# Two-layer graph network: first row tile normalized alone, first head's W1 as two transfers, edge transposes moved to the front

## What is computed

```python
h = jnp.maximum(_layernorm(x, axis=-1), 0.0)
x = x + _L0_gnn_ref(h, edge_index, L0_gnn_W1, ...)   # 4 heads of 512, attention, W2
h = jnp.maximum(_layernorm(x, axis=-1), 0.0)
x = x + _L1_gnn_ref(h, L1_gnn_W1, ..., edge_index)   # graph convolution
...
def _gat_layer(x, src, dst, W, a_src, a_dst, bias, concat):
    h = (x @ W).reshape(N, H, C)
    ...
```

## Time and profile before

| | |
|---|---|
| time, median of 3 runs | 1191.17 us |
| lowest, highest of the 3 | 1186.42 us, 1191.92 us |
| the profiled execution, its time | 1188.23 us |
| its span, from first to last instruction | 1186.5 us |
| TensorE busy | 1114.7 us, 94% of the span |
| VectorE busy | 836.6 us, 71% |
| ScalarE busy | 513.0 us, 43% |

### The profile page before, as it was taken

How to read it: one execution, slowest core, us unless ns; L and a number is a source line. 1 busy time by engine, 2 the same in 40 slices (tenths; PEclk the granted TensorE clock), 3 DMA queues, 4 the chain that set the end, 5 groups by cost and what they waited for, 6 DMA issues and landing times. The chain is left out here.

```text
span 1186.5 us, 17506 instructions
## 1 busy us (share of the span) xinstructions
PE 1114.7 (94%) x7124; PEld 1045.2 (88%) x7124; DVE 836.6 (71%) x1390; ACT 513.0 (43%) x1052; POOL 30.4 (3%) x40
## 2 busy tenths in 40 slices
PE   5999999999999999999999999739999899999998
PEld 5878886789989998999999999729999899889998
DVE  7998896899768886788768778679856623341263
ACT  4232322375547654556547654155445613431120
POOL 4200001020000000000000000000000000000000
PEclk9999999989999999999999999969999999999999
DMA  6133130021011100201020100013002300000321
GB/s 221 66 113 116 40 122 18 1 63 54 1 51 40 54 1 1 89 16 40 1 69 22 54 1 1 1 56 115 28 27 68 116 1 1 27 14 1 131 75 56
DMA packets 27618, 58.44 MB, mean 49 GB/s; under 512 B 3492, under 2 KB 6152, under 8 KB 27536
## 3 DMA queue, kind: packets, MB, share of 16 engines
q1 hardware_dynamic: 27344, 56.96, 14.5%
q10 hardware_dynamic: 192, 0.32, 0.1%
HBM read 41.73 MB, written 15.54 MB: 48 GB/s over the span
## 5 line engine op out<-in xcount | busy, mean ns | idle before, releaser
L1330 PE MATMUL banks<-hs,ring_hi 128*128 128x258 f32 (+1 forms) x1600 | 299.4, 288 | 2.8 <-DVE z L997 2.8
L1330 PEld LDWEIGHTS banks<-hs,ring_hi 128*128 128x128 f32 (+1 forms) x1600 | 247.9, 188 | 4.2 <-DVE z L997 3.0
L1330 PE MATMUL banks<-hs,ring_lo 128*128 128x258 f32 (+1 forms) x800 | 227.0, 284 | 0.0
L248 ACT ACTIVATE e<-banks,al 128x256 f32<-128x256 f32 (+1 forms) x500 | 193.9, 491 | 22.4 <-PE banks L233 22.4
L1330 PEld LDWEIGHTS banks<-hs,ring_lo 128*128 128x128 f32 (+1 forms) x800 | 150.9, 189 | 0.0
L256 ACT ACTIVATE ring_hi<-pf 128x512 fp32r<-128x512 f32 (+1 forms) x125 | 81.6, 653 | 159.8 <-DVE pf L267 156.6
L1358 PE MATMUL banks<-w_hi,oT_hi 128*128 128x384 f32 (+1 forms) x320 | 109.5, 342 | 12.7 <-DVE rows L1025 6.9
L265 DVE TENSOR_TENSOR e<-e 128x512 f32<-128x512 f32 (+1 forms) x125 | 84.5, 676 | 36.6 <-ACT e L248 36.4
L1358 PE MATMUL banks<-w_lo,oT_hi 128*128 128x384 f32 (+1 forms) x320 | 109.0, 341 | 0.0
L1358 PE MATMUL banks<-w_hi,oT_lo 128*128 128x384 f32 (+1 forms) x320 | 108.9, 340 | 0.0
L1204 PE MATMUL banks<-w_hi,xT_hi 128*128 128x512 f32 x240 | 97.4, 406 | 0.5 <-DVE w_lo L781 0.5
(11 more groups left out here) (262 smaller groups left out, 2109.7 us busy)
## 6 DMA issues: line engine op xcount, KB each, us to landing
h_scratch<-stage SPq DMA_DIRECT2D x30, 256.0 KB, 2.0
hs<-h_scratch SPq DMA_DIRECT2D x30, 256.0 KB, 2.9
w_st<-in_L_gnn_W SPq DMA_DIRECT2D x4, 1536.0 KB, 7.4
w_st<-in_L_gnn_W SPq DMA_DIRECT2D x16, 384.0 KB, 3.5
gw_st<-in_L_gnn_W SPq DMA_DIRECT2D x12, 384.0 KB, 3.8
xr<-in_x SPq DMA_DIRECT2D x9, 384.0 KB, 10.1
rows<-in_x SPq DMA_DIRECT2D x9, 384.0 KB, 3.2
x_scratch<-rows SPq DMA_DIRECT2D x9, 384.0 KB
```

The lines of the kernel that those rows point to most:

```text
L248: last = nc.scalar.activation(self.e[:, local % 2, a, i, 0:n], self.p_shift[:, a, 0:n], ACT.Exp, bias=scores[a][:, g * G + i:g * G + i + 1])
L1330: last = nc.tensor.matmul(p_a[0:m, dt, half, 0:HH], wt.ring[a][:, s // G, s % G, dt * P:dt * P + m], hs[:, s, b, half * HH:(half + 1) * HH ...
```

## The change

- `PARTS` becomes four groups: tile 0 alone, tiles 1 and 2, tiles 3 to 5, tiles 6 to 9. `factors` and `deviations` run once more.
- W1 of the first head comes in two transfers of three blocks each, of 768 KB. The first is issued behind row tile 0 and has a semaphore of its own (`w_front`), the second behind row tile 1; row tile 2 now follows both. The other heads keep one transfer.
- ACT's queue: the square root of tile 0 comes ahead of the edges' conversion; the root of tiles 1 and 2 stands between the fourth and the fifth block of W1.
- DVE's queue: the statistics and factors of tile 0, then tile 1, two low blocks of W1, tile 2, the low part of row tile 0, the factors of tiles 1 and 2, four low blocks, the low part of row tile 1, and only then `dest_spans`.
- PE's queue: the edges' transposes first, then those of tile 0; those of tile 1 come between the third and the fourth block of the first product.
- One semaphore (`picked`) is merged into another.

```diff
-                if t == 2:
-                    load_weights(sp, 0)
+                if t < 2:
+                    load_weights(sp, 0, slice(t * FRONT, (t + 1) * FRONT))
...
-PARTS = [(0, 3), (3, 6), (6, T)]
+PARTS = [(0, 1), (1, 3), (3, 6), (6, T)]
+FRONT = KD // 2
...
             def weight_hi(i, ks=range(KD)):
-                act.wait_ge(w_in, 16 * (i + 1))
+                if i == 0 and ks[0] < FRONT:
+                    act.wait_ge(w_front, 16)
+                else:
+                    act.wait_ge(w_in, 16 * (i + 1))
...
+            deviations(0)
             edges_float()
-            deviations(0)
-            weight_hi(0, range(0, 3))
+            weight_hi(0, range(0, FRONT))
             turned_hi(0)
-            weight_hi(0, range(3, KD))
+            weight_hi(0, range(FRONT, FRONT + 1))
+            deviations(1)
+            weight_hi(0, range(FRONT + 1, KD))
             turned_hi(1)
-            edges_out(e_src[:, :], e_dst[:, :], NCH, et_done)
-            deviations(1)
+            edges_out(e_src[:, :], e_dst[:, :], NCH, 1)
+            deviations(2)
...
-            row_parts(range(0, 3))
+            row_parts(range(0, 1))
             factors(0)
+            row_parts(range(1, 2))
+            weight_lo(0, range(0, 2))
+            row_parts(range(2, 3))
+            turned_lo(0)
+            factors(1)
+            weight_lo(0, range(2, KD))
+            turned_lo(1)
             dest_spans()
-            weight_lo(0, range(0, 3))
-            turned_lo(0)
-            weight_lo(0, range(3, KD))
-            turned_lo(1)
             row_parts(range(3, 6))
-            factors(1)
+            factors(2)
...
             pe.wait_ge(made, 12)
-            for t in range(2):
-                turn_rows(t)
             transpose_edges()
+            turn_rows(0)
             for n in range(FIRST):
-                tile(n)
+                if n == 0:
+                    tile(0, range(0, FRONT))
+                    turn_rows(1)
+                    tile(0, range(FRONT, KD))
+                else:
+                    tile(n)
```

More of the change, by code:

```diff
@@ L151, in build, with load_weights @@
         a_in = keep.enter_context(nc.semaphore("a_in"))
+        w_front = keep.enter_context(nc.semaphore("w_front"))
         tile_in = [keep.enter_context(nc.semaphore(f"tile_in{t}")) for t in range(T)]
-        def load_weights(sp, i):
+        def load_weights(sp, i, ks=slice(0, KD)):
             h = ORDER[i]
-            sp.dma_start(mem.w_st[:, :, :], W1.rearrange("(k p) n -> p k n", p=P)[:, :, h * HID:(h + 1) * HID]).then_inc(w_in, 16)
+            sp.dma_start(mem.w_st[:, ks, :], W1.rearrange("(k p) n -> p k n", p=P)[:, ks, h * HID:(h + 1) * HID]).then_inc(w_front if ks.start == 0 and ks.stop < KD else w_in, 16)
         def load_vectors(sp, i):
@@ L163, in build @@
         with ExitStack() as st:
-            first_layer(nc, st, mem, x, src, dst, W2, b1, as2, ad2, h_scratch, w_in, a_in, load_weights, load_vectors, tile_in)
+            first_layer(nc, st, mem, x, src, dst, W2, b1, as2, ad2, h_scratch, w_in, w_front, a_in, load_weights, load_vectors, tile_in)
         with ExitStack() as st:
@@ L288, in shift_parts, with first_layer @@
     nc.vector.tensor_tensor(parts[:, 2:4, :], shift[:, :, :], parts[:, 0:2, :].bitcast(fp32), ALU.subtract).then_inc(ready, 1)
-PARTS = [(0, 3), (3, 6), (6, T)]
+PARTS = [(0, 1), (1, 3), (3, 6), (6, T)]
+FRONT = KD // 2
 FIRST_COUNT = 9
-def first_layer(nc, st, mem, x, src, dst, W2, b1, as2, ad2, h_scratch, w_in, a_in, load_weights, load_vectors, tile_in):
+def first_layer(nc, st, mem, x, src, dst, W2, b1, as2, ad2, h_scratch, w_in, w_front, a_in, load_weights, load_vectors, tile_in):
     pb, sem = makers(nc, st)
@@ L377, in first_layer @@
     edges_out_done = sem("edges_out_done")
-    et_done = sem("edges_and_spans_turned")
+    et_done = sem("edges_turned")
     spread_ready = sem("spread_ready")
-    picked = sem("picked")
     red_ready = sem("red_ready")
@@ L572, in edges_float, with edges_out @@
                 nc.scalar.activation(e_f[:, :, :, :], e_i[:, :, :, :], ACT.Copy).then_inc(ef_ready, 1)
-            def edges_out(sources, dests, n, done):
-                act.wait_ge(done, 1)
+            def edges_out(sources, dests, n, turn):
+                act.wait_ge(et_done, turn)
                 nc.scalar.activation(sources, p_e[:, 0, 0:n], ACT.Copy).then_inc(edges_out_done, 1)
                 nc.scalar.activation(dests, p_e[:, 1, 0:n], ACT.Copy, scale=float(T)).then_inc(edges_out_done, 1)
+            deviations(0)
             edges_float()
-            deviations(0)
-            weight_hi(0, range(0, 3))
+            weight_hi(0, range(0, FRONT))
             turned_hi(0)
-            weight_hi(0, range(3, KD))
+            weight_hi(0, range(FRONT, FRONT + 1))
+            deviations(1)
+            weight_hi(0, range(FRONT + 1, KD))
             turned_hi(1)
-            edges_out(e_src[:, :], e_dst[:, :], NCH, et_done)
-            deviations(1)
+            edges_out(e_src[:, :], e_dst[:, :], NCH, 1)
+            deviations(2)
             for n in range(FIRST):
@@ L599, in _ @@
                 if n == 3:
-                    deviations(2)
+                    deviations(3)
                 if n == 6:
-                    edges_out(s_i[:, :], d_f[:, :], NW * FIX, picked)
+                    edges_out(s_i[:, :], d_f[:, :], NW * FIX, 3)
                 for g in groups_after(n):
@@ L877, in _ @@
             row_parts(range(8, T))
-            factors(2)
+            factors(3)
             turned_lo(5)
@@ L1179, in pick_chunks @@
                                                 start=j == 0, stop=j == EJ - 1)
-                last.then_inc(picked, 1)
+                last.then_inc(et_done, 1)
             def turn_rows(t):
@@ L1188, in turn_rows, with tile @@
                 last.then_inc(xt_done, 1)
-            def tile(n):
+            def tile(n, ks=range(KD)):
                 i, t = n // T, n % T
@@ L1196, in tile @@
                         pe.wait_ge(hlo_done, n - 1 - FIRST)
-                u = 0
-                for k in range(KD):
+                u = 3 * ks[0]
+                for k in ks:
                     if t == 0:
@@ L1208, in tile @@
                         last.then_inc(w_free, 1)
-                last.then_inc(h_ready, 1)
+                if ks[-1] == KD - 1:
+                    last.then_inc(h_ready, 1)
             def count(wd):
```

## The result

| | before | changed |
|---|---|---|
| median of 20 runs each | 1188.78 us | 1192.09 us |
| lowest, highest | 1186.15, 1193.9 us | 1190.62, 1196.69 us |
| span of the profiled execution | 1186.5 us | 1192.2 us |

The changed kernel takes 1.0024 [1.0014, 1.0035] times the time of before, some 2.9 us more: a loss that 20 runs resolve, and well inside the half per cent that counted as no change.

What follows compares the result with a forecast made beforehand. TensorE, busy 94% of the span, was taken as the bound. It would be 1.8 us late at tile 3 and another 1.1 at the fourth product, 2.9 in all: 1192.3 us against 1189.4, range 1187 to 1197.5.

Steps and rivals of the forecast that it cites:

- POOL's tile 1: POOL's normalization of tile 1, forecast to start at 15.7 and take 1.2 us.
- The statistics of tile 3: On DVE, the statistics of tiles 3 to 5 start at 22.3 instead of 18.42, 3.9 us later.
- The end of the chain: At tile 3's low part DVE is 3.9 us late, at 35.6; PE waits another 1.1 and is 2.9 late.
- Nothing gives it back: From 109 us on DVE waits for PE, so a late PE delays DVE alike and the lateness stays.
- the sum: The profiled execution's 1188.23 us plus 2.9 gives 1191.1; against the four known times' average of 1189.4 it is 1192.3.
- the new stall: PE, ready at 26 to 28.6, waits for POOL's tile 3 and starts its transposes at 29.1, 1.8 us late.
- The lead: PE starts the first product at 14.0 instead of 16.53, 2.5 us ahead, all idled away at tile 3.
- The rule on transposes: Transposes inside the first product could keep its second half at the slow pace, costing 1.8 us; the sum stays.
- both ends: The second product's end on PE, 26 at full rate or 28.6 with a low clock, both before 29.0.
- The lead is kept: Rival: tile 3 is normalized in time and PE's 2.5 us survive; -2 us, 1187.4; chance 0.10.
- Slower, by the clock: Rival: the clock falls after PE's idle at tile 3, PE 4.5 or 6.1 late, 1193.9 to 1195.5; chance 0.20.
- Absorbed: Rival: PE's later waits for DVE alone make the lateness good; result 0, 1189.4; chance 0.12.

Runs made afterwards that it cites:

- e3: The changed kernel with tile 3's statistics moved on VectorE ahead of tile 1's low part; 1.0005 times the kernel before.
- e2: The changed kernel with tile 1's transposes put ahead of the whole first product, which is in one piece again; 1.0026 times the kernel before.
- e9: The kernel before with only PE's new order (edges first, tile 1's transposes inside the first product); 1.0032 times the kernel before.
- e5: The changed kernel, VectorE relieved: tile 3's statistics fill its wait, dest_spans and maxima later, window products on POOL, last root earlier; 1.0002 times the kernel before.
- e1: The changed kernel with dest_spans moved on VectorE behind the low part of tile 2; 1.0022 times the kernel before.
- e6: The kernel before with VectorE relieved: window products on POOL, their maxima later, the last group's root earlier; 0.9998 times the kernel before.
- e7: The kernel before with tile 3's statistics computed twice, 1.3 us of added VectorE work; 1.0011 times the kernel before.
- e4: The changed kernel with the first head's W1 in one transfer again, behind row tile 2; 1.0043 times the kernel before.
- e8: The changed kernel with tile 3's statistics computed twice, 1.3 us of added VectorE work; 1.0026 times the kernel before.
- e10: The kernel before with 22 identity matmuls, results overwritten, ahead of PE's first transposes; 0.9999 times the kernel before.
- e11: e6 with 22 identity matmuls, results overwritten, ahead of PE's first transposes; 1.0006 times the kernel before.

## Why the prediction was right

| step of the prediction | forecast | measured |
|---|---|---|
| edges' transposes start | 8.0 | 7.58 |
| tile 1's, tile 2's statistics start | 8.7, 11.7 | 8.34, 11.46 |
| first product | 14.0 | 13.87 |
| POOL's tile 1: start, length | 15.7, 1.2 | 15.31, 2.40 |
| tile 1's transposes | 17.9 | 17.77 |
| low part of tile 1 | 20.2 | 19.52 |
| statistics of tile 3 | 22.3, 3.9 late | 21.67, 3.25 late |
| POOL's second group | 27.9 | 27.28 |
| transposes of tile 3, PE's lateness | 29.1, 1.8 | 28.32, 0.99 |
| fourth product, PE's lateness | 35.6, 2.9 | 34.78, 2.12 |
| what is late from then on | 2.9 | 2.08, from the twelfth product 1.66 |
| the time, and before | 1192.3 against 1189.4 | 1192.09 against 1188.78 |

**The mechanism held.** VectorE waits ahead of tile 1's low part, tile 3 is normalized late, PE idles its lead away and starts late twice. e3 (give VectorE 1.0 back, get 1.0), e2 (take 3.8 to 5.1 from PE, lose 0.7) and e9 (PE's order alone costs 2.7) each show a piece of it, and e5 shows that the stall goes when VectorE's load goes.

**The terms were too large.** *The statistics of tile 3* are 3.25 late, not 3.9: all landings of this profile came 0.3 us earlier, and tile 1's transposes, costed at the slow pace, ran at the full one, as the rate had doubled at 16.9. *The end of the chain:* VectorE's lateness was to arrive whole at the low part of tile 3. It arrived as 2.94 (33.70 against 30.76), since the kernel before had a wait of 0.33 of VectorE for ACT ahead of tile 2's low part (at 24.25) that the changed one has not, and PE's part of it as 2.12. *Nothing gives it back* was not quite so: 0.4 went between the eleventh and the twelfth product. PE waits there for `w_lo` of the next head, twice in the kernel before (0.25 and 0.28 us, and each time its next matmul starts some 0.4 late) and once in the changed one (0.29): one such stop less is the 0.4. The prediction saw no wait of PE between 70 and 109 us; these were there. So in the profile the change cost 1.7 us by VectorE's queue and not 2.9. That the time came out at +2.9 by the ratio does not confirm the 2.9 of the sum: the ratio's own interval is 1.7 to 4.2 us, and at equal clock it is 1.7 (0.65). What lies between 1.7 and 2.9 can be chance or a price in clock of the new stall; the mean clocks, 0.9817 in the changed kernel's runs and 0.9825 in the 99 of before, differ by less than their scatter resolves.

*The lead* was counted at the first product, as 2.5, with "the whole lead of 2.5 is idled away" and -2 us for the rival that keeps it. But tile 1's transposes were still owed there. By the prediction's own times PE was ready for tile 3 at 26 for 27.33, a lead of 1.3 at most; measured it was 2.0 at the second product, and it went into 2.87 us of idle and 0.99 of lateness. The sum did not use the lead, so the slip cost nothing.

**A size that was wrong without harm.** POOL's tile 1 was put at 1.2 us. Its group of two took 3.79 us, and the first alone 2.40, while VectorE made four low blocks of W1 beside it. One by one, POOL's tile 1 and the last of the four blocks:

```profile
15.31 2.40 POOL L526 TENSOR_SCALAR xr<-xr,norm_rstd,norm_nmr 128x768 f32<-128x768 f32 x1 [6.53 <-DVE norm_nmr L775]
16.94 1.31 DVE L787 TENSOR_TENSOR w_lo<-w_st,w_hi 128x512 fp32r<-128x512 f32 x1
```

POOL's tile 0, with no low block beside it, took 0.98; the three blocks ahead of the last took 0.68 to 0.69 each. The nine matmuls ended at 17.6 and PE waited 0.20 us more for tile 1. In e2, where nothing covered it, it ended the wait of 6.9 us. The Trainium skill ("SBUF — State Buffer", section "Who interferes with whom") says that a VectorE instruction with two inputs in SBUF contends with a GpSimd instruction that reads SBUF; `w_lo` is made from two such tiles, and the trace agrees.

**The rule on transposes.** The Trainium skill ("TensorE: Matmul & The Clock Gate", section "Part 4: PE-mode transpose") has transposes not counting as a busy array. By it, the split could hold the first product's second half at the slow pace. The runs do not settle it. With the split the pace doubled 3.0 us after the product's start in the changed kernel, 3.4 in e9 and 3.8 in e3, with the six transposes still to come, and 5.8 and 5.9 in e1 and e5, with them inside; with the product in one piece it was 2.5 in e2, 3.8 in the kernel before and 5.0 in e6 and e7. As the prediction had it, both ends fit ahead of the stall, so the sum stood.

**The rivals.** *The lead is kept* is excluded by the stall. *Slower, by the clock* asked for a fall behind the new stall. In the changed kernel's profile there was none after 2.87 us of idle; in e4 (2.6) and e8 (4.1) there was, worth 1.7 us each. So it is a real price of such a stall that this profile happened not to pay; how often the changed kernel's runs pay it was not measured, and the rival is not excluded for them. *Absorbed* had a fifth of its way: 0.46 of 2.12.

## What to carry to other kernels

Starting the bound engine earlier gains only what the engine that feeds it can follow. Before moving work forward, add up the feeder's queue to the next shared product, and look above all for a producer that is placed late in the bound engine's own order (here tile 1's transposes inside the first product), because the feeder stands still for it. A kernel of 1190 us whose runs scatter by 8 can still be read more finely: start times of the same product in both traces, to 0.3 to 0.5 us here, and spans compared at equal granted clock, to about 1 us with ten runs. Take that start time behind a point up to which both orders have done the same work.

## What the runs showed of the hardware

- The granted clock column reads 1.00 while matmuls of 512 columns start 0.43 us apart, in every profile ahead of the first rise (16 to 20 us in the kernel before). Up to there only the pace tells the level; falls that come later do show in the column.
- Length of idle alone did not decide a fall: none after 2.87 us (the changed kernel), one after 2.6 (e4) and one after a wait of 1.7 (e10), while e11 with a wait of 1.5 at the same place had none.
- One thousandth of mean clock is worth 0.7 to 0.8 us of span in this kernel. The runs' clocks lie between 0.974 and 0.987, which is most of their scatter: after the fit 1.3 to 1.5 us are left.
- POOL's normalization of a tile (128x768 floats) took 0.98 us with none of VectorE's `w_lo` or window products beside it. Beside four `w_lo` blocks it took 2.40, and of the four, 0.68 to 0.69 us each otherwise, the last took 1.31. In e5's group of three, whose window products are gone from VectorE, the three tiles took 3.32 us, in the changed kernel's 3.92.
- The pace doubled 2.5 to 5.9 us after the first product began, in the nine profiles named above, whose PE had done only transposes ahead of it.
